# Turning the selection counts by DMA instead of by TensorE in chunks 2 to 4 of a two-layer recurrent block

## The reference, cut to what matters

```
s  = xn @ (block-masked weight).T + bias            # 512 -> 512
inter = xn @ c1_w.T @ c2_w.T                        # 512 -> 16 -> 1792
blk = inter.reshape(tokens, 56, 32)                 # 56 segments of 32
idx = argmax(blk, -1) + arange(0, 1792, 32)         # one unit of each segment
h   = relu(einsum('bkm,bm->bk', w1[idx], xn))
g   = einsum('bk,bkm->bm', h, w2t[idx])
```

## Time and profile before

| | |
|---|---|
| median of 3 runs | 671.59 us (670.92 to 672.86) |
| the profiled execution | 671.89 us, span 670.1 us |
| PE busy | 638.2 us, 95% of the span |
| DVE busy | 449.9 us, 67% |
| POOL busy | 233.0 us, 35% |
| ACT busy | 213.8 us, 32% |
| granted PE clock, mean | 0.995 |

### The profile page before, as it was taken

One profiled execution on the slowest core, in us unless ns is written; L12 is line 12 of the kernel. 1 busy time (PEld: TensorE's weight loads), 2 busy tenths in 40 slices (PEclk: granted clock), 3 DMA queues, 4 the chain that ended last, 5 costly groups with the idle time before them and its releaser, 6 DMA issues.

```text
span 670.1 us, 8639 instructions
## 1 busy us (share of the span) xinstructions
PE 638.2 (95%) x3078; PEld 515.8 (77%) x3078; DVE 449.9 (67%) x716; ACT 213.8 (32%) x379; POOL 233.0 (35%) x185
## 2 busy tenths in 40 slices
PE   2599999999999999999999999999999999999997
PEld 2478788778788778788777788787878878887887
DVE  6977875597664597664597786664856667485633
ACT  2423333412122412122411233654146126413610
POOL 1516555360000360000390343464514342342441
PEclk9899999999999999999999999999999999999999
DMA  8940000040000040000052110013021013002001
GB/s 237 405 172 1 0 1 0 24 166 1 0 1 0 23 167 0 0 0 0 19 213 108 63 49 15 16 49 126 32 102 56 1 47 141 0 31 80 17 23 41
DMA packets 19535, 40.66 MB, mean 61 GB/s; under 512 B 2032, under 2 KB 2416, under 8 KB 18864
## 3 DMA queue, kind: packets, MB, share of 16 engines
q1 hardware_dynamic: 19504, 40.25, 16.9%
HBM read 31.85 MB, written 8.39 MB: 60 GB/s over the span
## 4 chain that ended last, share of the span: by engine, by line
PE 85%; DVE 8%; issue 3%; POOL 1%; ACT 1%; DMA 1%; SPq 0%; DVEq 0%; POOLq 0%; ACTq 0%
PE bank L410 76%; PE bank L344 2%; PE bank L1154 2%; PE bank L1135 1%; DVE counts L882 1%; DVE eq L872 1%; DVE seg_top L870 1%; PE bank L1286 1%; DVE ws_lo L935 1%; PE bank L1117 1%; PE bank L1249 1%; DMA x_tile<-in_x 1%; DVE h_lo L906 1%; POOL g_tile L390 1%; DVE ws_raw L930 1%
## 5 line engine op out<-in xcount | busy, mean ns | idle before, releaser
L410 PE MATMUL bank<-w_hi_t,h_hi 128*128 128x512 f32 x224 | 93.6, 418 | 1.5 <-DVE h_lo L906 1.5
L708 ACT ACTIVATE h_hi<-h 128x512 fp32r<-128x512 f32 x56 | 35.4, 632 | 176.4 <-DVE h L897 176.4
L882 DVE TENSOR_TENSOR_SCAN counts<-restart,eq 128x512 bf16<-128x512 bf16 (+1 forms) x64 | 87.4, 1365 | 2.0
L410 PE MATMUL bank<-w_lo_t,h_hi 128*128 128x512 f32 x224 | 87.9, 392 | 0.0
L410 PE MATMUL bank<-xT_hi,w_hi_t 128*128 128x512 f32 x224 | 87.6, 391 | 0.0
L410 PE MATMUL bank<-w_hi_t,h_lo 128*128 128x512 f32 x224 | 87.5, 390 | 0.0
L410 PE MATMUL bank<-xT_lo,w_hi_t 128*128 128x512 f32 x224 | 87.2, 389 | 0.0
L410 PE MATMUL bank<-xT_hi,w_lo_t 128*128 128x512 f32 x224 | 87.2, 389 | 0.0
L870 DVE TENSOR_REDUCE seg_top<-bank 128x16 f32<-128x512 f32 (+1 forms) x64 | 39.6, 619 | 67.8 <-PE bank L1135 67.8
L390 POOL TENSOR_TENSOR g_tile<-g_tile,s_tile 128x512 f32<-128x512 f32 x31 | 43.7, 1408 | 94.3 <-DVE g_tile L919 49.4
L376 POOL TENSOR_TENSOR rstd<-mean_var,eps 128x4 f32<-128x4 f32 x8 | 1.6, 202 | 173.9 <-DVE mean_var L370 173.9
(11 more groups left out here) (185 smaller groups left out, 1304.8 us busy)
## 6 DMA issues: line engine op xcount, KB each, us to landing
w_raw<-in_w SPq DMA_DIRECT2D x28, 256.0 KB, 9.5
x_res<-in_x SPq DMA_DIRECT2D x4, 1024.0 KB, 8.0
mid_state<-g_tile SPq DMA_DIRECT2D x16, 256.0 KB, 2.0
x_tile<-mid_state SPq DMA_DIRECT2D x4, 1024.0 KB, 7.4
x_res<-mid_state SPq DMA_DIRECT2D x4, 1024.0 KB, 5.5
out<-g_tile SPq DMA_DIRECT2D x15, 256.0 KB, 2.0
x_tile<-in_x SPq DMA_DIRECT2D x3, 1024.0 KB, 5.4
b_raw<-in_lora_b SPq DMA_DIRECT2D x2, 1024.0 KB, 4.9
```

The source lines that it names most:

```text
L410: last = nc.tensor.matmul(dst, a, b, start=(start and n == 0), stop=(stop and n == len(mms) - 1))
L708: nc.scalar.activation(h_hi[:, it % 2, :], h[:], ACT.Copy).then_inc(h_hi_done, 1)
L882: nc.vector.tensor_tensor_scan(counts[:, p % 2, tt, 0:PW[p]], restart[:, 0:PW[p]], eq[:, 0:PW[p]], 0.0, ALU.mult, ALU.add).then_inc(sel_co ...
```

## The change

In chunks 2 to 4 (c = 1 to 3) the counts are no longer turned by PE. `counts` is now one buffer [128, 4, 512] in SBUF, and a second tensor `first` [128, 2, 4, 512] holds the turned counts of two pieces, also in SBUF. After each scan of a token tile, SP issues one `dma_start_transpose` (a "turn") that brings up to 512 columns of this tile into `first[:, p % 2, :, rows(tt)]`. The mask on DVE reads `first` from SBUF; at every fourth unit tile it waits for the four turns of its piece (`ld_first`). A scan waits until the turn of the piece before has read its part of `counts`.

In chunk 1 PE turns the counts as before. The piece-0 turns of the next chunk stand in SP's queue between the row stores of the present one. In the head, PE makes the scores right after the `s` product of the same token tile (before, scores came one product later and those of the fourth tile after the first up product), and DVE does all four selections in the head.

In the last chunk the loads of the layer-2 weights stand between the turns, and ACT rounds `base_raw` and `wo_raw` one unit tile later.

```diff
-        counts = span_t.take("counts", [P, 2, TT, BANK], BF16)
+        first = span_t.take("first", [P, 2, TT, S], BF16)
+        counts = span_t.take("counts", [P, TT, BANK], BF16)
...
+            def turn(c, p, tt):
+                sp.wait_ge(sel_count, c * NSEL + p * TT + tt + 1)
+                sp.sem_inc(turns, 1)
+                sp.dma_start_transpose(first[:, p % 2, 0:PW[p] // P, rows(tt)], counts[:, tt, 0:PW[p]])\
+                    .then_inc(ld_first[tt], 16)
...
             def chunk(c, source, last):
                 if last:
                     sp.wait_ge(s0_done, CH * TT)
                     sp.dma_start(wqkv_raw[:], wqkv).then_inc(ld_wqkv, 16)
                     sp.dma_start(a_raw[:], a_w).then_inc(ld_wqkv, 16)
+                for tt in range(TT):
+                    turn(c, 1, tt)
+                next_rows(c, source)
+                if last:
                     sp.wait_ge(s_biased, CH * TT)
                     sp.dma_start(bias_a[:], bo.rearrange("(a n) -> a n", a=1).to_broadcast([P, D])).then_inc(ld_bo, 16)
+                for tt in range(TT):
+                    turn(c, 2, tt)
+                    if last and tt == 0:
+                        sp.wait_ge(up_done, (CH - 1) * IT + KD + 1)
+                        sp.dma_start(base_raw[:], base_w).then_inc(ld_base, 16)
+                        sp.dma_start(wo_raw[:], wo).then_inc(ld_base, 16)
+                for tt in range(TT):
+                    turn(c, 3, tt)
+                    if last and tt == 0:
+                        next_b(0)
+                if last:
+                    next_b(1)
+            def rows_out(c, place, to_next):
+                for tt in range(TT):
+                    if to_next:
+                        turn(c + 1, 0, tt)
+                    store_row(c, place, tt)
...
-                if it == KD + 3:
+                if it == KD + 4:
                     act.wait_ge(ld_base, 2 * 16)
...
             def select_count(c, p, tt):
                 dve.wait_ge(sel_eq, c * NSEL + n + 1)
-                if tt == 0 and p >= 2:
-                    dve.wait_ge(first_tr, c * IT + 4 * (p - 1))
+                if not opens(c):
+                    dve.wait_ge(ld_first[tt], (c * PIECES + p) * 16)
+                elif tt == 0 and p >= 2:
+                    dve.wait_ge(first_tr, 4 * (p - 1))
...
                     dve.wait_ge(relu_done, c * IT + it + 1)
-                    dve.wait_ge(first_tr, c * IT + it + 1)
-                    nc.vector.scalar_tensor_tensor(h[:], first, 1.0, h[:], ALU.is_equal, ALU.mult).then_inc(h_masked, 1)
+                    if opens(c):
+                        dve.wait_ge(first_tr, it + 1)
+                        which = first_bank
+                    else:
+                        if it % 4 == 0:
+                            for tt in range(TT):
+                                dve.wait_ge(ld_first[tt], (c * PIECES + it // 4 + 1) * 16)
+                        which = first[:, it // 4 % 2, it % 4, :]
+                    nc.vector.scalar_tensor_tensor(h[:], which, 1.0, h[:], ALU.is_equal, ALU.mult).then_inc(h_masked, 1)
...
-                s_product(c, 0)
-                s_product(c, 1)
-                select(c, 0, 0)
-                s_product(c, 2)
-                select(c, 0, 1)
-                s_product(c, 3)
-                select(c, 0, 2)
+                for tt in range(TT):
+                    s_product(c, tt)
+                    select(c, 0, tt)
...
-                    transpose_counts(c, it - 1)
+                    if first:
+                        first_transpose(it - 1)
```

More of the change, by code:

```diff
@@ L269, in block_mask_ffn_then_attention_lora_kernel @@
         first_tr = sem("first_tr")
+        turns = sem("turns")
+        ld_first = [sem(f"ld_first_{tt}") for tt in range(TT)]
         up_done = sem("up_done")
@@ L400, in rows, with opens @@
             return slice(tt * P, (tt + 1) * P)
+        def opens(c):
+            return isinstance(c, int) and c == 0
         def s_bank(c, tt):
@@ L422, in block_mask_ffn_then_attention_lora_kernel @@
         mask_bank = banks[5]
-        first = banks[7][:].bitcast(BF16)[:, 0:S]
+        first_bank = banks[7][:].bitcast(BF16)[:, 0:S]
+        first_counts = [counts, first[:, 1]]
         NSEL = PIECES * TT
@@ L463, in _, with store_row, next_b, next_rows @@
                 sp.dma_start(bqkv_col[:], bqkv.rearrange("(j p) -> p j", p=P)).then_inc(ld_l1_small, 16)
-            def chunk(c, source, last):
+            def turn(c, p, tt):
[3 more added lines that the diff above has]
+                    .then_inc(ld_first[tt], 16)
+            def store_row(c, place, tt):
+                sp.wait_ge(rows_done, c * TT + tt + 1)
+                sp.dma_start(place[:, tt, :], g_tile[:, tt, :]).then_inc(st_rows, 16)
+            def next_b(i):
+                part = slice(i * KE // 2, (i + 1) * KE // 2)
+                sp.wait_ge(down_done, (CH - 1) * IT + part.stop)
+                sp.dma_start(b_raw[:, part, :], lora_b[:, part, :]).then_inc(ld_b[i], 16)
+            def next_rows(c, source):
                 sp.wait_ge(xT_tr, c * TT + TT)
@@ L472, in chunk @@
                 sp.dma_start(x_res[:], x_rows[c]).then_inc(ld_res, 16)
+            def chunk(c, source, last):
                 if last:
@@ L886, in head @@
                 t_rest(c)
-                for tt in range(TT - 1):
+                for tt in range(TT):
                     select(c, 0, tt)
             def body(c, last):
-                select(c, 0, TT - 1)
                 for it in range(IT):
@@ L1146, in up_product, with first_transpose @@
                                       for k in range(KD)]).then_inc(up_done, 1)
-            def transpose_counts(c, it):
-                pe.wait_ge(sel_count, c * NSEL + (it // 4 + 1) * TT)
+            def first_transpose(it):
+                pe.wait_ge(sel_count, (it // 4 + 1) * TT)
                 if it:
-                    pe.wait_ge(h_masked, c * IT + it)
+                    pe.wait_ge(h_masked, it)
                 for tt in range(TT):
-                    last = nc.tensor.transpose(first[:, rows(tt)], counts[:, it // 4 % 2, tt, rows(it % 4)], ident_bf[:])
+                    last = nc.tensor.transpose(first_bank[:, rows(tt)], first_counts[it // 4 % 2][:, tt, rows(it % 4)], ident_bf[:])
                 last.then_inc(first_tr, 1)
@@ L1178, in body @@
                     up_product(c, 0)
-                    select(c, 0, 3)
                 for it in range(1, IT + 1):
```

24 lines of the change are left out of this document (11 added, 13 removed).

## The result

| kernel | median us | runs from to | ratio to before, 95% interval |
|---|---|---|---|
| before, beside it | 672.23 | 670.92 to 673.28 | |
| changed | 664.45 | 663.29 to 666.39 | 0.9888 (0.9857 to 0.992) |
| changed, once more, with the experiments | 663.19 | 662.82 to 664.95 | 0.9873 (0.9854 to 0.9892) |

The changed kernel is faster by 1.1 to 1.3%, 7.8 us in the first comparison. The first profiled execution took 666.39 us (span 664.6), the highest of its four. The second took 662.92 us (span 661.0). Where the two differ, both are shown.

A forecast was written before the change was run, and what follows sets the result against it. PE was taken to bound chunks 2 to 4. Gains of 3.85 us each in chunks 2 and 3 and 0 in chunk 4, together 7.7 off 671.6, gave 663.9, stated as 664.0 us; range 657.5 to 672.5.

The forecast's parts named there:

- The bound: In chunks 2 to 4 PE sets the pace; work taken from it shortens the time one for one.
- The transposes, 4.2 us per chunk: PE's unit tiles: 14 groups of four transposes per chunk, 0.30 us each, are saved.
- The body's start: Each chunk's first mask waits for its turn; PE waits 1.85 us, 0.35 more than before.
- The other turns: Turns of pieces 1 to 3 are hidden: latency up to about 6.5 us free, 3.7 for piece 3.
- Tile 4 of the last chunk, 1.0 us: Beside POOL's subtraction, less DVE reserve (0.3 us) and a slower SBUF mask (0.7) cost 1.0 together.
- `b_raw`, 2.25 + 0.6 us: End of chunk 4: load behind last turn makes PE 2.25 us late; 0.6 of saved transposes is lost too.
- Chunks 2 and 3, -3.85 each; chunk 4, 0: Sum per chunk: 4.2 less 0.35 in chunks 2 and 3; chunk 4's 3.6 is used up by its costs.
- rivals 2 to 4: By turn latency: 2, 1.7 us, 657 us (chance 0.16); 3, about 5, no change (0.11); 4, beyond 5.3, slower (0.18).
- L: Time for a DMA turn to land after issue, the one unknown; taken as 3.1 us.
- rival 1: The forecast itself: turn latency between 2.2 and 4 us, kernel at 667 to 661 us; chance 0.55.
- rival 3: No change: a turn takes about 5 us, the gain gone at 4.9, time 671.6 us; chance 0.11.

The follow-up runs named there:

- experiment 3: Changed kernel without the DMA turns of chunks 2 to 4 and the waits for them, masks not the reference's: 658.76 us, ratio 0.9811.
- experiment 1: The changed kernel measured again with no edit, on the chip of three other kernels: 663.19 us, ratio 0.9873.
- experiment 6: Changed kernel with the second half of `b_raw` issued behind the second turn of piece 3 instead of the fourth: 660.19 us, ratio 0.9811.
- experiment 4: Changed kernel with three tiny stores ahead of the last turn of piece 0 in chunks 2 to 4, delaying it: 675.34 us, ratio 1.0056.
- experiment 8: Changed kernel with POOL's four bias additions of a head held back until `h_lo` of the body's first tile: 670.37 us, ratio 0.9963.
- experiment 10: Changed kernel with the last turn of piece 0 split in two, the first mask's block ahead: 663.45 us, ratio 0.9866.

## Why the prediction was right

664.0 us was forecast and 664.45 and 663.19 were measured. The mechanism held: PE's work for the transposes went, and the turns' latency showed only at the body starts. That the time agrees so closely is in part luck. The transposes were worth more than forecast and the turn landed sooner, while a late scan in chunk 3 and falls of the clock, for which the prediction has no term, took about as much back. Point by point:

- **The bound.** Right. Taking the transposes from PE and putting dead ones back moves the time by what they cost PE, and without turns chunk 2 is PE's work to within 0.02 us.
- **The transposes, 4.2 us per chunk.** Too small by 0.55. Chunk 2 took 100.59 us before, 99.09 without the 1.50 lost at its body start, and 94.34 without transposes, turns or waits (experiment 3): 4.75 us for 14 groups. A group is worth 0.36 us in wide tiles and 0.29 in the last piece. In a wide tile the forecast's 0.30 left out that behind a group the down product's matmuls were also slower, 0.232 us apart (150.67 to 151.83 in five steps in the kernel before) instead of 0.227 (161.22 to 163.94 in twelve).
- **The body's start.** A little less than forecast: PE loses 1.68 us at the first one (1.85 forecast, 1.5 before), 1.3 at the second by the same working. The last scan ends 18.25 us after the chunk's start (18.1 forecast), and the down product starts at 149.65 (149.8 forecast, counted from this execution's start of the chunk). Scan's end to mask is 3.1 us in chunk 2 and 2.5 in chunks 3 and 4, where the forecast had 3.3 with its wake-ups. The turn itself lands 2.3 us after its issue (minimum and median), not 3.1. Which wait PE shows was wrong: it is `eq`, because the selection of piece 1 reads the same bank in turn and stands on DVE behind the mask. It hides most of the wait for `h_lo`, so the sum didn't change.
- **The other turns.** Hidden, as forecast, though some take 6.8 us to land. (For piece 3 the forecast had a slack of 3.7 us; its terms as written, 8.3 - 1.7 - 2.7, leave 3.9. Nothing hangs on this.)
- **Tile 4 of the last chunk, 1.0 us.** Half right. In sum it is 0.9: over an undisturbed tile the tile was 1.7 us longer before (7.73 and 6.02) and is 2.6 longer in experiment 1 (8.29 and 5.66). A mask from SBUF beside POOL was indeed the cost, but at 3.9 us, not at the +0.7 of `h_lo`; the scan beside it lost its own 3 us, since it now starts just ahead of POOL. The Trainium skill describes this in "SBUF — State Buffer", section "SBUF: two separate sides": DVE with two inputs in SBUF and GpSimd reading SBUF exclude each other for the whole of an instruction, and the one that starts first goes first. The rows agree: the scan that was first took 1.22 us, the mask behind it ended 0.55 us after POOL's instruction (364.22 + 3.92 = 368.14, and 363.12 + 4.47 = 367.59), about its own 0.69 us.
- **`b_raw`, 2.25 + 0.6 us.** Right in the first term: with the load moved (experiment 6) chunk 4 is 2.24 us shorter, and ACT's wait for it was 2.39 us. The rest of that experiment's 3.0 isn't `b_raw`'s: 0.9 is chunk 3's scan.
- **Chunks 2 and 3, -3.85 each; chunk 4, 0.** Measured -4.6, -4.0 and +0.2 in the execution in which the clock held, and -4.4, -4.0 and +3.2 in the other. In chunk 2 this is 4.75 for the transposes less 0.1 more at the body start. In chunk 3 it would be -4.9 but for the late scan of experiment 6 (0.9). Chunk 4 has one cost that the forecast lacks: PE waits 0.63 us for `h_lo` at 348.10, a tile behind a scan that took 2.17 us while POOL made `pick`; before, the scan beside it took 2.06, and PE didn't wait.
- **The rivals.** The DMA's turn decides by its latency, as rivals 2 to 4 had it, but their prices are too low on the slow side. Masks that come 1.3 to 1.6 us later at the three body starts (experiment 4) cost 12.2 us, not the 4.5 of one for one. A turn lands at 2.3 us, so this is like an L of 3.6 to 3.9, for which rival 1 has a gain of 5 to 6 us; measured, the kernel is then slower than the one before. The point from which the change gains nothing lay below that, not at the L = 4.9 of rival 3. The forecast held because the turn was fast enough, by a margin smaller than it stated.
- **The Trainium skill's figure for the DMA's turn.** The Trainium skill, "VectorE: DVE Perf Modes", section "The three transpose paths", gives 1309 ns for one block; four in a row are 5.2 us by an estimate from this figure. No row bears this out for one instruction of four blocks: 2.3 us to land is the median, and the wait is the same for one block as for four.

## What to carry to other kernels

Where one engine is the limit and never idle, even 0.3 us operations are worth moving to an idle resource, if the consumer has slack longer than the new path. So count first the places without slack, move their producer earlier, and look at what the new transfers push back in their queue. Don't price a new wait of the matrix engine at its length alone: behind waits of 1.85 us and more the clock fell in some executions of this kernel, and each fall cost about as much again. Compare windows of stages that an edit touches and of those that it doesn't before giving it the whole difference of two medians. An operand that moves from PSUM to SBUF can change whom its reader has to wait for.

## What was not expected of the hardware

- **The clock behind single waits.** PE ran at 1.2 GHz for some 3 to 4 us behind waits of 1.85 and 1.89 us (experiment 8), 2.18, 2.42 and 2.52 us (late turn), 2.33 us (first execution of the changed kernel), 2.56, 2.79, 2.99, 3.08 and 3.26 us in the kernels above. It did not behind other waits of 1.89 (experiment 8, chunk 4), 2.15, 2.33, 2.53, 2.81, 2.87, 2.96 and 3.01 us. So the length of the wait alone doesn't decide; what does was not found. One such fall costs 1.5 to 2 us, as much as the wait; behind the 3.26 us the clock stayed low for longer (0.58, 0.50, 0.50 and 0.71 from 351 to 359 us), 3.4 us of work.
- **A tie between two engines.** Where DVE's scan and POOL's multiplication start within 0.02 us of each other, which one is lengthened differs from execution to execution, and it is worth 0.9 us of the kernel (experiment 6).
- **A turn's fixed cost.** SP is occupied for 1.12 to 1.30 us by one turn, whatever its number of blocks (one turn of 1.57 us in experiment 1 and one of 1.39 in experiment 10 apart), and for 0.33 to 0.57 us by a plain store of 256 KB.
- **Small packets.** The kernel after moves 25072 packets under 512 B, the one without turns 2032. No wait was found that comes from it; `b_raw` lands in 5.1 us instead of 4.9.
